# Gated cross-attention and mixture-of-experts block on one core: router logits in column groups, and a reordered tail

## The reference

```python
x = x + tanh(g_xattn) * xattn(layernorm(x), ctx, ctx)      # 16 heads of 16, softmax, output projection
x = x + tanh(g_ffn) * ffn(layernorm(x))
# ffn, per token:
scores = softmax(xf @ w_router)                            # 8 experts
top-2 experts keep their scores as weights cw
moe    = sum_e cw_e * (silu(xf @ w1_e) * (xf @ w3_e)) @ w2_e
shared = (silu(xf @ ws1) * (xf @ ws3)) @ ws2
out    = shared / 3 + moe * 2 / 3
```

## Time and profile before

| what | value |
|---|---|
| median of 3 runs | 824.37 us (824.17 to 826.52) |
| profiled execution | 821.54 us |
| its span, first to last instruction | 819.8 us, 19446 instructions |
| mean granted TensorE clock | 0.994 |
| busy, share of the span | PE 94%, PEld 84%, DVE 66%, POOL 53%, ACT 50% |
| chain that ended last, share by engine | PE 51%, POOL 14%, DMA 13%, issue 9%, DVE 7%, ACT 4% |

### The profile page before, as it was taken

How to read it: one execution, slowest core, us unless ns; L and a number is a source line. 1 busy time by engine, 2 the same in 40 slices (tenths; PEclk the granted TensorE clock), 3 DMA queues, 4 the chain that set the end, 5 groups by cost and what they waited for, 6 DMA issues and landing times.

```text
span 819.8 us, 19446 instructions
## 1 busy us (share of the span) xinstructions
PE 771.5 (94%) x6977; PEld 688.4 (84%) x6978; DVE 543.3 (66%) x1118; ACT 413.4 (50%) x690; POOL 432.0 (53%) x486
## 2 busy tenths in 40 slices
PE   4889999999999999988998999999999999999997
PEld 4766777777777766568998999999999999999996
DVE  5677789998888898946564444444444444456787
ACT  5767776777777776742334324343333343333331
POOL 5633446666666655466571566656757584236000
PEclk9999999999999999999999999999999999999999
DMA  6855556766666653253487343324333422218522
GB/s 205 275 179 164 187 182 229 227 225 216 211 213 208 206 175 124 96 183 130 146 231 265 75 128 85 113 68 119 99 106 82 121 53 75 54 57 327 219 81 74
DMA packets 129102, 127.34 MB, mean 155 GB/s; under 512 B 55184, under 2 KB 110992, under 8 KB 129040
## 3 DMA queue, kind: packets, MB, share of 16 engines
q1 hardware_dynamic: 114896, 80.34, 32.8%
q0 software_dynamic: 14144, 46.19, 16.1%
HBM read 75.32 MB, written 50.91 MB: 154 GB/s over the span
## 4 chain that ended last, share of the span: by engine, by line
PE 51%; POOL 14%; DMA 13%; issue 9%; DVE 7%; ACT 4%; SPq 2%; POOLq 1%; ACTq 0%; DVEq 0%
PE bank L561 6%; POOL w_l L1610 6%; PE bank_ss L613 5%; PE bank L563 5%; PE bank L562 5%; DMA y_d<-y_s,y_rows 5%; PE bank L642 5%; DMA y_rows<-xs_d 4%; PE bank_sm L626 4%; PE bank_sm L561 3%; PE bank_sm L562 2%; PE bank_sm L563 2%; PE bank_ss L561 2%; PE bank L649 2%; PE bank_ss L563 2%
## 5 line engine op out<-in xcount | busy, mean ns | idle before, releaser
L1247 DVE TENSOR_REDUCE row_max<-bank_sm 128x4 f32<-128x1024 f32 x124 | 151.5, 1222 | 38.2 <-PE bank_sm L626 36.8
L952 ACT ACTIVATE probs_T<-bank_ss 128x1024 f32<-128x1024 f32 x123 | 126.4, 1027 | 18.8 <-PE bank_ss L613 18.5
L1226 DVE TENSOR_TENSOR gT_l<-gg,gT_h 128x1024 fp32r<-128x1024 f32 x49 | 66.7, 1360 | 103.1 <-ACT gT_h L1083 103.1
L561 PE MATMUL bank_sm<-xg_h,w_h 128*128 128x256 f32 x400 | 115.1, 288 | 4.5 <-DVE xg_l L1226 4.4
L561 PE MATMUL bank<-w_h,gT_h 128*128 128x256 f32 x392 | 111.4, 284 | 3.2 <-DVE gT_l L1226 3.2
L562 PE MATMUL bank_sm<-xg_h,w_l 128*128 128x256 f32 x400 | 114.4, 286 | 0.0
L563 PE MATMUL bank_sm<-xg_l,w_h 128*128 128x256 f32 x400 | 114.3, 286 | 0.0
L561 PE MATMUL bank_ss<-xg_h,w_h 128*128 128x256 f32 x400 | 113.2, 283 | 0.0
L562 PE MATMUL bank_ss<-xg_h,w_l 128*128 128x256 f32 x400 | 112.9, 282 | 0.0
L563 PE MATMUL bank_ss<-xg_l,w_h 128*128 128x256 f32 x400 | 112.9, 282 | 0.0
L562 PE MATMUL bank<-w_h,gT_l 128*128 128x256 f32 x392 | 110.9, 283 | 0.0
(11 more groups left out here) (203 smaller groups left out, 1951.7 us busy)
## 6 DMA issues: line engine op xcount, KB each, us to landing
qk_d<-qk_s SPq DMA_DIRECT2D x64, 256.0 KB, 3.0
w_raw<-wall POOLq DMA_DIRECT2D x27, 512.0 KB, 3.9
k<-qk_d SPq DMA_DIRECT2D x48, 256.0 KB, 4.1
q<-qk_d SPq DMA_DIRECT2D x48, 256.0 KB, 4.6
xq<-xs_d SPq DMA_DIRECT2D x140, 64.0 KB, 2.2
y_pairs<-y_d POOLq DMA_DIRECT2D x16, 512.0 KB, 8.8
x<-x SPq DMA_DIRECT2D x16, 256.0 KB, 4.7
c_s<-ctxT SPq DMA_DIRECT2D x16, 256.0 KB, 3.0
```

The lines of the kernel that those rows point to most:

```text
L561: pe.matmul(out, ah, bh, start=first and k == 0, stop=False)
L952: act.activation(pT[:, 2 * (pv % 4):2 * (pv % 4) + 2, :].rearrange("p h t -> p (h t)"), exp_bank(V.b, pv)[:, :], ACT.Exp, scale=D ** -0.5) ...
L1226: return v.tensor_tensor(dst, ps, high.bitcast(F32), ALU.subtract)
L1247: v.tensor_reduce(mx[B.slot][:, :, :].rearrange("p t (r q) -> p r t q", r=2)[:, :, :, p], max_bank(B.b, p)[:, :].rearrange("p (r t k) -> p ...
```

## The change

Seven things change.

1. **Router logits, batches 0 to 9** (`thin`). At p = 1 four matmuls take the router's weights, padded from 8 to 32 columns, as the loaded operand and stream 128 tokens each; the four results (two token halves times two halves of the features) lie in four 32-partition groups of one bank. ACT copies that bank (`logits_turned`), and at p = 2, behind the values, one float32 matmul with a constant 128x16 selection matrix adds the feature halves and turns the result. DVE's `best_two` goes from ahead of row maximum 2 to ahead of row maximum 3. Batches 10 to 15 keep the old form.
2. **Warm-up matmuls** of 512 columns in half the number, and in pass i = -1 (`Eb.b == R`) the statistics of batch 3 ahead of the first row maximum.
3. **Tail, PE, ACT, DVE.** Logits of batches 13 and 14 go to another bank, so that `project_out` waits no more; ACT copies the last head group ahead of the first silu; `turn_norm(x15)`, `logits(x15)` and `rank(x15)` each go one step later.
4. **Tail, POOL.** Both `root` calls go ahead of the `cut` that stood before them.
5. **Routed tiles** are turned into a PSUM bank, not into SBUF, and the first one ahead of `gated(5)`.
6. **Residual rows** come in four loads of four batches, behind experts 0 to 3.
7. **End.** Expert results of batches 14 and 15 are added to the residual rows during tiles 11 to 14 (`add_pair`), so that one instruction for batch 14 and two for batch 15 are left.

```diff
+        def thin(batch):
+            return batch.b < THIN
...
+            def logits_apart(S3):
...
+                for j in range(TC * EC):
+                    t, k = j // EC, j % EC
+                    r = pe.matmul(lgT_p[LW * j:LW * (j + 1), :], wr_s[:, k, :], xn2T[:, k, t * P:(t + 1) * P], start=True, stop=True)
+                r.then_inc(lgT_ps, 1)
+
+            def logits_joined(S3):
+                pe.wait_ge(lgT_ok, S3.n(1, 1))
+                pe.matmul(lg_thin, lgT_s[:, :], K[:, C_SEL:C_SEL + TC * NX], start=True, stop=True).then_inc(lg_ps, 1)
...
                     if p == 1 and S3:
-                        logits(S3)
+                        (logits_apart if thin(S3) else logits_whole)(S3)
...
+                    if p == 2 and S3 and thin(S3):
+                        logits_joined(S3)
...
-            logits(x13)
-            pe.wait_ge(lgc_ok, x13.n(1, 1))
+            logits(x13, lg_tail)
             project_out(x14)
...
             down(0, SHARED)
+            up1(2, SHARED)
             turn_norm(x15)
-            up1(2, SHARED)
-            logits(x15)
             up3(2, SHARED)
+            logits(x15, lg_p)
+            down(1, SHARED)
             rank(x15, rk_tail)
-            down(1, SHARED)
...
+            head_out(x15, 3)
             silu(0)
-            head_out(x15, 3)
...
+                    if p == 0 and Eb and Eb.b == R:
+                        stats_ahead()
+                        variance_ahead()
-                    if p == 2 and S3:
-                        best_two(S3)
+                    if p == 3 and S3 and thin(S3):
+                        best_two(S3, lg_thin)
+                        masks(S3)
...
-                v.transpose(xrT[:, :, :].rearrange("p c (t q) -> p c t q", q=QD),
+                v.transpose(psX[:, :].rearrange("p (c t q) -> p c t q", c=EC, q=QD),
...
             g_low(4)
+            v.wait_ge(pos_ok, NB)
+            turn_rows(EARLY)
             gated(5)
             x_low_routed(EARLY)
...
+            PAIR_AT = {NB - 5: (NB - 1, 0), NB - 4: (NB - 1, 1), NB - 3: (NB - 2, 0), NB - 2: (NB - 2, 1)}
...
                     gated(end + (j - EARLY))
+                    if j in PAIR_AT:
+                        add_pair(*PAIR_AT[j])
                     g_low(end + (j - EARLY))
...
+            root(bmv2, rstd2, var2_ok, x14, rstd2_ok)
             cut(1, 0, which=(0,))
-            root(bmv2, rstd2, var2_ok, x14, rstd2_ok)
...
             cut(2, 1)
-            po.wait_ge(x2_st, NB * 16)
-            po.dma_start(x2a[:, :, :], x2_d.rearrange("b p d -> p b d")).then_inc(x2_in, 16)
-
...
                 with po.Fori(tb + 1, te) as g:
                     scatter_y(g)
+                if e < X2_PARTS:
+                    n = NB // X2_PARTS
+                    po.wait_ge(x2_st, NB * 16)
+                    po.dma_start(x2a[:, e * n:(e + 1) * n, :], x2_d[e * n:(e + 1) * n].rearrange("b p d -> p b d")).then_inc(x2_in, 16)
```

More of the change, by code:

```diff
@@ L51 @@
 WP = 3
+X2_PARTS = 4
 PVW = 32
@@ L106, in constants @@
     c[:, C_T3:C_T3 + NST] = c[:, C_T2:C_T2 + NST] + 1
+    for j in range(TC * EC):
+        for n in range(NX):
+            c[LW * j + n, C_SEL + (j // EC) * NX + n] = 1.0
     return c
@@ L844, in _ @@
             up1(1, SHARED)
-            logits(x14)
-            pe.wait_ge(lgc_ok, x14.n(1, 1))
+            logits(x14, lg_tail)
             project_out(x15)
@@ L972, in norm_out, with logits_turned @@
                 from_bank(xn2T, T1, xn2T_ps, S3, lg_ps, S3.n(), xn2T_ok)
+            def logits_turned(S3):
+                act.wait_ge(lgT_ps, S3.n(1, 1))
+                moved(act, lg_ps, S3.n())
+                act.activation(lgT_s[:, :], lgT_p, ACT.Copy).then_inc(lgT_ok, 1)
             def router_exp(S3):
@@ L1028, in behind @@
                         norm_out(S3)
+                    if p == 1 and S3 and thin(S3):
+                        logits_turned(S3)
                     if p == 2 and A:
@@ L1357, in behind @@
                         list_slots(S4)
-                    if p == 1 and Eb:
-                        moved(v, xn_ok, Eb.n())
-                        mean_and_variance(bst, bmv)
-                        add_eps(bmv, var1_ok)
-                    if p == 2 and S3:
+                    if p == 1 and Eb and Eb.b != R:
+                        variance_ahead()
+                    if p == 2 and S3 and not thin(S3):
                         masks(S3)
@@ L1435, in _ @@
             x13, x14, x15 = (Batch(NB - k) for k in (3, 2, 1))
-            best_two(x13)
+            best_two(x13, lg_tail)
             masks(x13)
@@ L1447, in _ @@
             gated(0)
-            best_two(x14)
+            best_two(x14, lg_tail)
             masks(x14)
@@ L1459, in _ @@
             g_low(1)
-            best_two(x15)
+            best_two(x15, lg_p)
             masks(x15)
+            x_low_shared(3, 3)
+            gated(2)
             positions(x15, rk_tail)
             list_slots(x15)
-            x_low_shared(3, 3)
-            gated(2)
+            g_low(2)
             v.wait_ge(cnt_ps, 1)
```

98 lines of the change are left out of this document (63 added, 35 removed).

## The result

The changed kernel is slower, by about half a per cent. Its median is 829.36 us (825.13 to 833.19, 20 runs) against 824.93 us for the kernel before on the same chip (821.74 to 831.37, 20 runs); the ratio is 1.0048 with a 95% interval of 1.0029 to 1.0066. The profiled execution took 827.34 us, its span is 825.5 us (before: 819.8), and the mean granted TensorE clock is 0.986 (before: 0.994).

A forecast was written before the change was run, and what follows sets the result against it. PE bounds the attention and expert stages; its idle times between mostly end with late DVE instructions. Terms sum to -17.25 us, from 821.54 to 804.3, plus 2.8 for the median: 807.1 us, range 802.5 to 815.0.

The forecast's parts named there:

- batch 15's half tile: Tail: ranks and scatters of batch 15 come a half tile, about 3 us, later, at no cost.
- Thin logits: Ten attention passes: column-group matmuls save PE 0.25 us per batch, -2.5 us for ten.
- Start: Before the first row maxima: batch 3's statistics and the aggregation go into DVE's wait, -1.0 us; warm-ups 0.
- Tail and first tile: Tail, -7.75 us from removed PE waits and clock recovery; first routed tile, -1.8 us from an earlier transpose.
- both waits for `lgc_ok`: Tail: two PE waits of 0.76 us go because the logits have another bank, -1.5 us.
- batch 15's norm: Tail: PE's wait for the normed batch 15 goes, with `up1` of tile 2 as cover besides, -2.37 us.
- root of batch 14: Tail: POOL's root ahead of the cut removes PE's wait for the normed batch 14, -1.56 us.
- The clock's -1.35: Tail: without the last idle time, the reduced clock in the 4 us behind it goes, -1.35 us.
- Residual rows, the four issues: Expert stage: no 4 MB load ahead of the third routed tile, -3.7 us; four load issues at expert changes, +2.4 us.
- End: Kernel's end: most additions of batches 14 and 15 move into earlier tiles, -2.9 us.
- The tail's idle time finds another owner: Rival: DVE's low parts hold PE; half the tail's and first tile's gains come back, +4.8, 811.9 us; chance 0.16.
- My slower case: Rival: four loads hold up `y_rows` at expert changes, +31.4 in place of +2.4, 836.1 us; chance 0.03.

The follow-up runs named there:

- run 3: Changed kernel with seven of the eight clearing stores placed after the second routed tile's load; ratio 1.0047 to the kernel before.
- run 10: Changed kernel with old logits, cuts between scatters, batch 15's steps at old places, and clearing stores except list 1's moved later; ratio 0.9823 to kernel before, 810.31 us.
- run 4: Changed kernel with batch 15's steps back at their old places on PE and DVE; ratio 0.9999 to the kernel before.
- run 7: Changed kernel with POOL's cuts between the two scatters of a batch and list_slots of batch 14 right behind its positions; ratio 0.9949 to the kernel before.
- run 1: Changed kernel with the thin batches' masks behind row maximum 3 again; ratio 0.9997 to the kernel before.
- run 8: Changed kernel with masks behind row maximum 3, thin batches' rank at p = 4, batch 15's steps at old places, cuts between scatters; ratio 0.9884 to the kernel before.
- run 6: Changed kernel with the logits of all batches in the old form; ratio 0.9901 to the kernel before.
- run 12: Changed kernel with old logits, cuts between scatters, batch 15's steps at old places, plus old warm-ups and batch 3 statistics between maxima; ratio 0.9846 to kernel before.
- run 2: Changed kernel with both POOL roots behind the cuts again; ratio 1.0021 to the kernel before.
- run 11: Changed kernel with old logits, cuts between scatters, batch 15's steps at old places, and residual rows in one 4 MB load; ratio 0.9924 to kernel before.

## Why the prediction was wrong

**The step that failed first** is in the tail: "The ranks and scatters of batch 15 come later by a half tile, about 3 us, and the first routed load follows them; it had some 14 us in hand before its turn on DVE, so this costs nothing." The 14 us were the first load's, and they did cover it. The second load has another chain, that of the table above, and no such slack: before, it was turned at 425.10, and a turned tile reaches PE in 2.1 us (441.36 to 443.49), so only 3.7 us were left until PE began it at 430.91. The last scatter became 10.7 us later. Of these, 7.6 were there when the tail began (340.23 and 347.86), and PE shared them; 3.0 arose in the tail, so the 3 us were right in size. They were not batch 15's half tile, though: DVE had its row numbers 51.6 us behind the beginning of the tail before (391.86) and 51.0 now (398.87). The 3.0 are 1.2 of POOL's queue, which went from batch 14's scatters straight to batch 15's, and 1.8 of waiting for batch 15's first scatter to land (3.41 for 1.57).

What the prediction never set against the slack is its own gain: PE, freed of its waits, came to the first routed tile 5.9 us earlier behind the beginning of the tail. So the lead fell by 8.9 us. The way from the last scatter to the second tile's turn grew by 5.6 (27.3 to 32.9), and 8.9 + 5.6 - 3.7 = 10.8 is PE's wait. That the clearing stores are in that way is shown by runs 3 and 10, that an earlier scatter shortens the wait by runs 4 and 7 (9.2 and 5.6 us less). Why the way is longer in all changed kernels, by 2.2 to 5.6 us, stays open. Cost: +10.9 us, and 2.6 us of half clock on the tile behind.

**Thin logits.** The matmul terms were right in sum: 0.91 - 0.36 - 0.24 = 0.31 saved, start to start, where I took 1.06 - 0.54 - 0.27 = 0.25. No row here shows a charge of its own for the change of array shape. What failed is the sentence "`best_two` with the masks goes behind row maximum 2, where DVE otherwise waits for PE". DVE's idle time there was 0.34 and 0.52 us a pass, the pair needs some 1.3, and 2.3 with the contention. Of the +4.7 us in ten passes, 4.15 are the masks' place (run 1), and with all of it mended the thin form still loses 0.2 us in ten passes or 0.4 (runs 8, 1 against 6). Run 8's row shows PE waiting for the row maximum behind the masks; that the later result loads DVE where DVE is the limit is the reading that fits, not a separate test.

**Start.** The 0.8 to 1.0 us of the statistics is there (run 12) and does not reach the end. The +1.4 of the ledger need not be the change's: the changed kernels of runs 2, 3, 4 and 7 have the same start, and their fourth turned maximum lies between 96.44 and 100.62 us. In the profiled execution of the changed kernel PE stood idle for 2.61 us for a transfer of q and had 0.78 of the clock for 5 us behind it; in run 3 with the same code it was 1.34 us and 1.00. The +1.5 of the last passes is likely of the same kind: the last three turned maxima stand 18.6 and 17.8 us apart in it, 17.5 and 17.5 in runs 2, 4 and 7, as before.

**Tail and first tile.** Gone as predicted: both waits for `lgc_ok`, the last head group's, batch 15's norm, the first routed tile's 1.80. Mis-sized: root of batch 14, -1.56 predicted, which gave +0.5 and a new wait of 1.01 behind it. The root did move, and the norm began 3.5 us earlier behind the beginning of the tail. But PE came 2.3 us earlier too, since the waits ahead of it were gone, and the cut beside the norm took 1.7 (2.44 for 0.74, back at 0.74 in run 7): 1.56 - 3.5 + 2.3 + 1.7 = 2.06. The clock's -1.35 was not gained either: 0.83 between 370 and 380 us.

**Residual rows, the four issues.** Gross gain underestimated (run 11), charge not seen in the changed kernel but at 2.7 to 3.4 us in eight of its edits; together -3.8 for -1.3, though half clock worked against it. An issue took 0.81 us, where I took 0.6. The waiting tile of the earlier trace rows, called the third routed one there and in the prediction, is the fourth: the turns before are at 418.83, 425.10, 436.07 and 448.53.

**End.** -3.1 for -2.9: right, term and mechanism, by the rows above; no run takes this part back by itself, nor the earlier turn of the first routed tile.

**The rivals.** "The tail's idle time finds another owner" was the right family, but I bounded it by half of the tail's gain. What came was a wait larger than all of those removed. My slower case hung on the four loads; they cost PE nothing to speak of here and at most 3.4 us at one change of expert in the other runs, far from four times 7.85. That the kernel came out slower has another cause, and none of the rivals followed the scatters to the second load.

## What to carry to other kernels

Slack belongs to one consumer: before moving a producer, follow its chain to the second and third consumer as well, with the transfers that stand between them, and set what makes the consumer earlier against what makes the producer later. A DVE instruction is not free because it fits in a gap: see what POOL does in the gap's new place. Bulk transfers that nobody waits for yet, such as clearing stores, belong behind the loads that the fastest engine will ask for next.

## What the runs showed of the hardware

- A DVE TENSOR_TENSOR of 128x32 took 1.24 us instead of 0.18 beside a POOL subtraction, a TENSOR_SCALAR pair of 128x256 took 2.44 instead of 0.74 beside POOL's cast and subtraction. Moving the DVE instruction (run 1) or POOL's cut (run 7) by one place brought the short time back.
- A block of eight rows of 128 columns in four column groups of 32 held PE for 0.36 us, two thirds of the 0.54 that I took.
- Clearing stores of 514 KB took 12.8 us in the median on POOL's queue (10.3 before), and a tile's load in four parts of 64 KB, asked for in their midst, some 20 us.
- Idle times of 1.68 and 1.01 us a short way apart were followed by a granted clock of 0.83 from 370 to 380 us (run 1), 0.72 and 1.01 by 1.00 there (run 6).
